# One ring of eight PSUM banks for the products of both layers, in place of a ring of five and a ring of three

## The reference, cut to what matters

```
x = x + A(layernorm(x), adj)   # 12 heads of 32: q, k, v; scores*scale + 2*adj; softmax; p@v; @Wo + bo
x = x + B(layernorm(x))        # 3 experts of 128: q, k (512-wide products), v and a gate;
                               # expert 0: q convolved over 3 tokens; softmax; weighted by the gate; @Wp + bp
```

## Time and profile before

| | |
|---|---|
| median of 3 runs | 2309.33 us (2308.97 to 2310.41) |
| the profiled execution | 2309.91 us, of which the span of the trace is 2308.1 us |
| PE busy | 2243.7 us, 97% of the span |
| DVE busy | 1899.6 us, 82% |
| ACT busy | 1503.0 us, 65% |
| POOL busy | 1096.8 us, 48% |
| granted TensorE clock, mean | 0.993 of 2.4 GHz |

### The profile page before, as it was taken

The page is one execution under the profiler, slowest core; times in us unless marked ns, Lnnn a source line. Parts: engine busy times, 40 slices in busy tenths (PEclk is TensorE's granted clock), DMA queues, the critical chain, the costliest instruction groups (busy, mean ns, idle before and its releaser), DMA issues.

```text
span 2308.1 us, 51446 instructions
## 1 busy us (share of the span) xinstructions
PE 2243.7 (97%) x16902; PEld 1605.2 (70%) x16902; DVE 1899.6 (82%) x7397; ACT 1503.0 (65%) x5290; POOL 1096.8 (48%) x1351
## 2 busy tenths in 40 slices
PE   5799999999999999999999999999999999999988
PEld 3476677766777766777766777766777767777666
DVE  6688888888888888888888888888888888888884
ACT  3567666677666676666676666676666776666763
POOL 2454454454454544454544554544554544544542
PEclk9899999999999999999999999999999999999999
DMA  5221122221122211222221222221222211222200
GB/s 171 60 54 52 44 74 74 74 50 46 53 74 74 74 47 45 58 74 74 63 55 41 65 74 74 57 54 42 71 75 74 51 55 45 74 74 74 50 12 28
DMA packets 142265, 143.20 MB, mean 62 GB/s; under 512 B 16816, under 2 KB 141360, under 8 KB 142000
## 3 DMA queue, kind: packets, MB, share of 16 engines
q1 hardware_dynamic: 138480, 137.18, 22.0%
q10 hardware_dynamic: 3520, 2.73, 0.4%
HBM read 39.18 MB, written 25.17 MB: 28 GB/s over the span
## 4 chain that ended last, share of the span: by engine, by line
PE 76%; DVE 17%; issue 2%; ACT 1%; SPq 0%; DMA 0%; POOL 0%; DVEq 0%; ACTq 0%
PE A_bank L463 29%; PE B_bank L463 24%; PE A_bank L534 6%; DVE raw_score L857 5%; PE B_bank L553 4%; PE A_bank L546 3%; PE A_bank L521 3%; PE B_bank L528 3%; DVE smax L864 3%; DVE V L846 3%; PE B_bank L538 2%; PE B_bank L500 2%; DVE g_tmp L794 1%; DVE q2raw L782 1%; PE A_bank L500 1%
## 5 line engine op out<-in xcount | busy, mean ns | idle before, releaser
L983 POOL TENSOR_TENSOR S<-S,rowf 128x512 f32<-128x512 f32 x384 | 389.0, 1041 | 699.4 <-DVE rowf L883 699.4
L642 ACT ACTIVATE S<-raw_score,smin 128x128 f32<-128x128 f32 x1536 | 593.4, 391 | 147.1 <-DVE smin L857 146.6
L857 DVE CUSTOM_DVE_ANT_0 raw_score<-A_bank,adj,s_unit 128x128 f32<-128x128 f32 x1536 | 444.9, 346 | 19.9 <-PE A_bank L521 19.9
L642 ACT ACTIVATION_READ_ACCUMULATOR S<-raw_score,smin 128x1 f32 x1536 | 292.2, 190 | 0.0
L656 ACT ACTIVATE PT<-A_bank 128x512 f32<-128x512 f32 x384 | 216.7, 592 | 76.4 <-PE A_bank L534 76.4
L864 DVE TENSOR_REDUCE smax<-raw_score 128x4 f32<-128x512 f32 x384 | 258.7, 681 | 0.3
L988 POOL TENSOR_TENSOR S<-S,row2f 128x384 f32<-128x384 f32 x128 | 105.9, 827 | 302.9 <-DVE row2f L891 300.6
L534 PE MATMUL A_bank<-ident,S 128*128 128x128 f32 x1536 | 216.7, 274 | 5.2 <-POOL S L983 5.1
L534 PEld LDWEIGHTS A_bank<-ident,S 128*128 128x128 f32 x1536 | 182.2, 142 | 25.7 <-issue 5.5
L660 ACT ACTIVATE yT_hi<-B_bank 128x384 fp32r<-128x384 f32 x128 | 62.1, 486 | 177.6 <-PE B_bank L553 177.6
L649 ACT ACTIVATE S<-S,s2min 128x128 f32<-128x128 f32 x384 | 148.9, 390 | 18.7 <-DVE s2min L868 18.6
(11 more groups left out here) (169 smaller groups left out, 6375.4 us busy)
## 6 DMA issues: line engine op xcount, KB each, us to landing
xin<-in_x SPq DMA_DIRECT2D x32, 768.0 KB, 4.6
Qs<-q_hi SPq DMA_DIRECT2D x256, 96.0 KB, 2.2
out<-x1res SPq DMA_DIRECT2D x128, 192.0 KB, 1.9
Ks<-k_hi SPq DMA_DIRECT2D x252, 96.0 KB, 2.7
Qs<-q_lo SPq DMA_DIRECT2D x128, 96.0 KB, 2.2
Ks<-k_lo SPq DMA_DIRECT2D x126, 96.0 KB, 2.2
adj<-in_adj SPq DMA_DIRECT2D x31, 256.0 KB, 3.5
S<-in_wq SPq DMA_DIRECT2D x1, 576.0 KB, 5.7
```

Of the source, the lines that this page charges most:

```text
L642: ins = nc.scalar.activation(S[b % 2][:, h, :], raw_score[c][:, j, :], ACT.Exp, bias=smin[b % 2][:, h:h + 1], scale=-1.0, accum_out=ssum[b ...
L857: ins = nc.vector.tensor_tensor_reduce(raw_score[c][:, j, :], src[:, j * T:(j + 1) * T], adj2[:, b, :], s_unit[:], 3.0e38, ALU.add, ALU.mi ...
L983: nc.gpsimd.tensor_tensor(S[b % 2][:, hs, :], S[b % 2][:, hs, :], rowf[b % 2][:, hs].unsqueeze(2).broadcast_to([P, HPC, T]), ALU.mult).the ...
```

## The change

All eight banks form one ring. The products of both layers and of the `W` steps take the banks in turn in the order of PE's list, and each waits for the evacuation of the product eight places back in that list, whichever layer it is of. The orders of the steps are untouched on every engine. The two `W` products of the start, which had fixed banks, get theirs from the ring and are waited for by a semaphore of the weight scaling.

```diff
-A_RING, B_RING = 5, 3
+BANKS = 8
...
-        bank = {s: [ctx.enter_context(nc.psum_tensor(f"{s}_bank{k}", [P, 512], F32)) for k in range(RING[s])]
-                for s in "AB"}
+        bank = [ctx.enter_context(nc.psum_tensor(f"bank{k}", [P, 512], F32)) for k in range(BANKS)]
...
-        ring = {s: [at for at in program["pe"] if at[0][0] == s] for s in "AB"}
-        ring_place = {at: n for s in "AB" for n, at in enumerate(ring[s])}
+        ring = program["pe"]
+        ring_place = {at: n for n, at in enumerate(ring)}
 
         def bank_of(step, g):
-            return bank[step[0]][ring_place[step, g] % RING[step[0]]]
+            return bank[ring_place[step, g] % BANKS]
...
         def wait_bank(eng, step, g):
 
-            n = ring_place[step, g] - RING[step[0]]
-            if n >= 0:
-                wait_evacuated(eng, *ring[step[0]][n])
+            n = ring_place[step, g] - BANKS
+            if n >= 0 and ring[n][0][0] == "W":
+                _, kind, part, _ = ring[n][0]
+                eng.wait_ge(tops if kind == "turn" else wscale_ready, part + 1)
+            elif n >= 0:
+                wait_evacuated(eng, *ring[n])
```

More of the change, by code:

```diff
@@ L65 @@
 MASKED = 1.0e30
-A_RING, B_RING = 5, 3
+BANKS = 8
 EVAC = {"hT": "dve", "qk": "act", "v": "dve", "score": "dve", "turn": "act", "mix": "dve", "proj": "dve"}
-RING = {"A": A_RING, "B": B_RING}
 FIRST_STEPS = {
@@ L472, in do @@
                 if stage == "W":
+                    wait_bank(pe, step, g)
                     n = scale_part[b].stop - scale_part[b].start
@@ L475, in do @@
                         pe.wait_ge(maxima, (2, 6)[b])
-                        nc.tensor.transpose(bank["B"][0][0:n, 0:P], wmax[:, scale_part[b]],
+                        nc.tensor.transpose(bank_of(step, g)[0:n, 0:P], wmax[:, scale_part[b]],
                                             ident[:]).then_inc(maxima_turned, 1)
@@ L479, in do @@
                         pe.wait_ge(tops, b + 1)
-                        nc.tensor.matmul(bank["B"][1][:, 0:n], top_col[0:n, b:b + 1].broadcast_to([n, P]),
+                        nc.tensor.matmul(bank_of(step, g)[:, 0:n], top_col[0:n, b:b + 1].broadcast_to([n, P]),
                                          ident[0:n, 0:n], start=True, stop=True).then_inc(tops_spread, 1)
@@ L707, in weight_scales @@
                 dve.wait_ge(maxima_turned, part + 1)
-                nc.vector.tensor_reduce(top_col[0:n, part:part + 1], bank["B"][0][0:n, 0:P], AXX,
+                nc.vector.tensor_reduce(top_col[0:n, part:part + 1], bank_of(("W", "turn", part, 0), 0)[0:n, 0:P], AXX,
                                         ALU.max).then_inc(tops, 1)
                 dve.wait_ge(tops_spread, part + 1)
-                link_scale(nc.vector.tensor_scalar(wtop[:, cols], bank["B"][1][:, 0:n], TINY, None, ALU.max))
+                link_scale(nc.vector.tensor_scalar(wtop[:, cols], bank_of(("W", "spread", part, 0), 0)[:, 0:n], TINY, None, ALU.max))
                 link_scale(nc.vector.tensor_scalar(wexp[:, cols], wtop[:, cols].bitcast(I32), EXP_BITS, None,
```

## The result

The kernel with one ring took 2580.61 us in the median (2577.95 to 2581.11, 4 runs), the kernel before 2309.15 us beside it (2307.24 to 2310.41, 4 runs). The ratio is 1.1174, with a 95% interval of 1.116 to 1.1188: 271.5 us slower. The forecast was 2605, in a range of 2560 to 2640.

A forecast was written before the change was run, and what follows sets the result against it. PE was taken as the bound, its work laid end to end in rounds of 69.74 us; 30 x (6.74 + 0.49 + 2.49) + 5 - 1 = 295.6 us more gave 2605 us, range 2560 to 2640.

The forecast's parts named there:

- The wait of B.qk.0: In each full round PE waits at B.qk.0 until DVE has read A.v.2: 6.74 us, bounds 6.0 to 7.0.
- A.turn.1.0: PE waits there for the drain of A.score.2.2, instead of at A.hT.2: 0.49 us a round, bounds 0.3 to 0.6.
- The clock: After the wait at B.qk.0 PE's clock falls to half speed in each round: 2.49 us lost, bounds 1.5 to 3.7.
- The first and last rounds: Next to last round 5 us lost (3 to 7), last nothing, start 1 us gained (0 to 6).
- Rival 1: The clock stays at full speed through the wait at B.qk.0: 2530 us, up to 2563; chance 0.06.
- Rival 2: DVE's B.conv is held up by POOL's bias instruction, so PE waits at B.v.1, about 1 us a round: 2635; chance 0.08.
- Rivals 3 and 4: 3: DVE reads A.v.2 before PE arrives, 2294 us, chance 0.02; 4: PE's list holds the wait elsewhere, no own chance.
- What would show it right: Some 31 PE waits for V near 200 us, rounds of 79 to 80 us, one clock fall each, smin waits at A.turn.1.0.

The follow-up runs named there:

- e1: The changed kernel with 28 extra matmuls on PE right before the wait of B.qk.0 in thirty rounds, results never read: 2531.04 us.
- e2: The kernel before, with its rings of five and three, and one added wait of B.qk.0 until DVE has read A.v.2: 2576.29 us.
- e3: The changed kernel with DVE's reads of A.v.2 and A.v.3 moved up behind A.v.1: 2325.62 us.
- e9: The changed kernel with DVE's read of A.score.2.2 moved ahead of B.gate.1: 2576.23 us.
- e6: The changed kernel with POOL's residual of B moved ahead of A.ln1: 2580.27 us.
- e11: The changed kernel with three extra matmuls of 384 columns ahead of A.score.0.0 in 28 rounds: 2603.51 us.
- e5: The changed kernel with DVE's reads of A.v.2 and A.v.3 moved only ahead of A.ln1: 2526.17 us.

## Why the prediction was right, and where it was off

**The wait of B.qk.0 (6.74 us).** Right, to 0.01: the excess in e1, where the clock plays no part, is 6.73. That DVE's run up to `A.v.2` hangs on PE's own earlier products held: in the changed kernel `A.v.2` is drained 10.06 us after its end, in the kernel before as well. e2 shows that the wait suffices, e3 that without it the time is back.

**A.turn.1.0 (0.49).** 0.97 more there and 0.53 less at `A.hT.2`: 0.44. The step was right, the size taken from start to start was a little high.

**The clock (2.49, bounds 1.5 to 3.7).** The mechanism was right: one fall in each round, after the wait, paid in full by PE. Its size was the term that was off: 1.58 us, near the low bound. That is 30 x 0.91 = 27 us, more than the whole distance between 2605 and 2581. The step that failed is "an average over thirty falls will lie near the middle". The falls were not thirty draws. They all came at the same place of the round, so the loss was the same each time, and no mean over unequal falls of the start and the end could give it. Nor is 1.58 what a wait of this length costs: behind the same 6.73 us the loss was 2.02 us a round in e2 and 2.54 in e9, which is close to the 2.49 taken. That the total still fell into the range is owed to bounds wide enough to hold all of these.

**The first and last rounds.** 5 for the end and 1 gained at the start. Measured from `A.score.0.0` of group 31 to the last product, the end grew from 107.4 to 114.5 us, 7 more; the start up to `A.score.0.0` of group 1 is 104.1 against 103.7. Over all the traces that start differs by up to 2.3 us, with no order by the rings, so no gain from the room of eight banks can be seen there. With 30 x (6.73 + 0.44 + 1.58) = 262.5 the sum comes to 262.5 + 7.1 + 0.5 = 270.1; the spans of the two profiled executions differ by 2578.3 - 2308.1 = 270.2.

**Rival 1, the clock holds.** Excluded by the rows at 0.50. Its price, 2530, was that of e1, 2531: what it described is what happens if PE has work in the wait. The further wait of up to 1.1 us a round at `B.v.1` that it reckoned with did not come: in e1 `A.score.1.2` was read 0.88 us before `B.v.1` started.

**Rival 2, the convolution meets POOL.** What it said of DVE happened: 3.48 us for an instruction of 0.75, and free only when POOL's had ended. That it costs nothing was right as well: DVE's read of `A.score.1.2` ended 0.71 us before `B.v.1` started, and e6, without the collision, has the same time (there it ended 0.88 us before). That this is also the 0.7 of the forecast is luck: from the start of `B.qk.0`, both PE's way to `B.v.1` and DVE's way to that read were 0.9 us shorter than reckoned. At a loss of 1.5 the prediction let PE wait for 0.3 us; the loss was 1.58 and PE did not wait. The rule of the shared port pair in the Trainium skill ("SBUF — State Buffer", section "Terms"), cited beside this rival, agrees with the two traces: DVE's instruction began 0.5 us after POOL's and ended 0.55 us after it, and took 0.75 us in e6, where POOL's was over before.

**Rivals 3 and 4** fell with the new line in the waits.

**What would show it right.** 31 waits for `V`, 204 us in total, those for `smin` at `A.turn.1.0` in place of `A.hT.2`, and a mean clock of 0.95 came as said. DVE was idle ahead of the convolution, but for 3.67 us where some 2 were said, and in the middle rounds it did not wait at `B.v.0`: the convolution, held up by POOL, ended after that product was made. The round of 79 to 80 us did not come either, for the reason above.

## What to carry to other kernels

A common ring of buffers pairs each product with the one that lies a fixed number of places back, and it is as slow as the occupant that is read last. Before merging or resizing rings, lay the new pairs over the old trace: for each, compare when the bank is drained with when PE comes to it, and then mend the late reader (here two words moved in DVE's list, into time in which DVE was idle) rather than the ring. When PE waits once in every pass, price the slow clock behind the wait too (here waits of 4.5 and 6.7 us each had a slow stretch behind them, those of 0.3 and 0.8 us had none); and as long as the clock falls in each pass, don't trust the measured worth of any other small change.

## What the runs showed of the hardware

The loss to the clock can adjust itself to the loop. Three kernels, whose rounds would be 76.91, 76.47 and 75.94 us long at full clock (69.74 plus their waits: the changed kernel, e2 and e9), all ran rounds of 78.51 us. The slow stretches lasted equally long and followed each other at that same distance, and what differed was how much of one PE spent waiting and how much working: 3.1, 4.0 and 5.2 us. Half of that is what they lost.

They came to 78.51 us from both sides. In the changed kernel the first full rounds took 79.29, 78.91, 78.71 and 78.59 us, in e9 78.35, 78.22, 78.37 and 78.43. The stretches at 0.50 stood 78.51 us apart even then, and PE's work in them (first column behind the comma) went towards the 3.1 and 5.2 us of the later rounds. The changed kernel, then e9:

```profile
195.60:202.30 6.70, 3.93 (x10) 1.46 (x11) 4.29 (x18) 0.00 (x0) 6.33 (x9) 0.50 0.00 0
274.10:280.80 6.70, 3.51 (x9) 1.31 (x10) 4.67 (x21) 0.00 (x0) 5.92 (x9) 0.50 0.00 1
352.60:359.30 6.70, 3.30 (x8) 1.20 (x9) 4.84 (x23) 0.00 (x0) 5.70 (x8) 0.50 0.02 4
```

```profile
194.50:201.20 6.70, 4.59 (x11) 1.60 (x12) 3.63 (x17) 0.53 (x1) 6.36 (x10) 0.50 0.00 0
273.00:279.70 6.70, 4.87 (x12) 1.80 (x13) 3.34 (x16) 0.81 (x2) 6.36 (x11) 0.50 0.00 1
351.50:358.20 6.70, 5.00 (x12) 1.80 (x13) 3.22 (x16) 0.94 (x2) 6.36 (x11) 0.50 0.02 4
```

One round near the end of e9 took 78.67 us; the stretch at 0.50 in the round after it came 78.51 us after the last one all the same, and rounds of 78.43 and 78.47 us brought the loop back. So in these kernels the falls of the clock come at instants that a longer or shorter round does not move, and the loop falls into step with them: a round that starts late for that step has less of PE's work in its slow stretch and loses less, one that starts early has more in it and loses more. What sets the distance of 78.51 us no run here shows. A round of 77.40 us (e11) did not settle on one length but ran through four, and one of 74.66 (e5) settled into pairs of unequal rounds; that the same falling into step explains these two as well was not tested.
